# Earlier last loads, rested coefficient places and reordered adds at the end of a graph network's edge loop

## What the kernel computes

```python
msg = sum over b of (h[src] @ weight[b]) * w_comp[etype][:, b]     # 8 bases
x1  = layernorm(x + relu(segment_sum(msg * norm, dst) + bias))
rst = (1 + eps) * x1 + segment_sum(x1[src] + edge_attr, dst)
h   = relu(batchnorm(rst @ W1 + b1))                              # over all nodes
out = layernorm(x1 + h @ W2 + b2)
```

## Time and profile before

| What | us |
|---|---|
| median of 3 runs | 603.0 |
| lowest and highest | 601.1 and 605.9 |
| the profiled execution | 599.79 |
| its span | 598.0 |
| PE busy | 500.1 |
| DVE busy | 466.3 |
| POOL busy | 400.9 |
| mean granted PE clock | 0.905 of full |

### The profile page before, as it was taken

How to read it: one execution, slowest core, us unless ns; L and a number is a source line. 1 busy time by engine, 2 the same in 40 slices (tenths; PEclk the granted TensorE clock), 3 DMA queues, 4 the chain that set the end, 5 groups by cost and what they waited for, 6 DMA issues and landing times. The chain is left out here.

```text
span 598.0 us, 12928 instructions
## 1 busy us (share of the span) xinstructions
PE 500.1 (84%) x3981; PEld 425.1 (71%) x3981; DVE 466.3 (78%) x1835; ACT 219.9 (37%) x325; POOL 400.9 (67%) x434
## 2 busy tenths in 40 slices
PE   3779678898787987878978987968799999887995
PEld 2459578677677686766766876767788998875675
DVE  5999999999998697977599886798853564647566
ACT  8914546454333342333343342342400000002386
POOL 7777777777777777777777777777777777730000
PEclk9996988897877977879986997998999999898999
DMA  5423866576665665676666875685875596824003
GB/s 140 126 55 89 280 186 195 163 257 188 197 199 140 205 179 190 197 221 194 194 194 219 261 228 195 207 275 183 256 251 173 181 298 175 229 62 145 2 2 108
DMA packets 102010, 108.20 MB, mean 181 GB/s; under 512 B 11430, under 2 KB 89239, under 8 KB 101939
## 3 DMA queue, kind: packets, MB, share of 16 engines
q1 hardware_dynamic: 82658, 77.81, 39.8%
q0 software_dynamic: 13312, 27.29, 16.7%
q10 hardware_dynamic: 5968, 2.24, 1.5%
HBM read 81.74 MB, written 25.56 MB: 179 GB/s over the span
## 5 line engine op out<-in xcount | busy, mean ns | idle before, releaser
L862 POOL DMA_INDIRECT gathered_flat<-in_x_dram,src_i x402 | 385.2, 958 | 122.5 <-issue 90.2
L955 ACT ACTIVATE adj_flat<-psum 128x500 f16<-128x500 f32 (+1 forms) x208 | 127.4, 612 | 231.2 <-PE psum L1214 222.3
L1190 PE MATMUL psum<-weighted,gathered_flat 128*128 128x96 f32 (+1 forms) x808 | 143.9, 306 | 26.0 <-DMA gathered_flat<-in_x_dram,src_i 25.9
L1183 PEld LDWEIGHTS psum<-hot,attrs 128*128 128x128 f32 x832 | 147.7, 215 | 12.6 <-issue 9.7
L1190 PEld LDWEIGHTS psum<-weighted,gathered_flat 128*128 128x128 f32 x808 | 124.3, 215 | 30.5 <-DMA gathered_flat<-in_x_dram,src_i 30.4
L1681 DVE TENSOR_SCALAR etype_hot<-iota_key,key_t 128x300 f16<-128x300 f16 (+1 forms) x416 | 137.0, 331 | 0.0
L1183 PE MATMUL psum<-hot,attrs 128*128 128x12 f32 (+1 forms) x832 | 133.3, 237 | 2.4 <-DVE weighted L1562 2.4
L1214 PE MATMUL psum<-etype_hot 128*128 128x300 f16 (+1 forms) x416 | 131.3, 343 | 2.5 <-DVE etype_hot L1681 2.4
L1678 DVE TENSOR_SCALAR etype_hot<-iota_key,gathered_flat 128x128 f16<-128x128 f16 x416 | 106.4, 256 | 20.5 <-PE psum L1214 15.2
L1810 DVE TENSOR_TENSOR sums_flat<-psum,sums_flat 128x180 f32 x208 | 71.0, 341 | 24.6 <-PE psum L1183 3.9
L1758 DVE TENSOR_TENSOR sums_flat<-psum,sums_flat 128x132 f32 x160 | 45.0, 291 | 49.4 <-PE psum L1281 23.9
(11 more groups left out here) (168 smaller groups left out, 388.5 us busy)
## 6 DMA issues: line engine op xcount, KB each, us to landing
attrs<-in_edge_attr_dram SPq DMA_DIRECT2D x51, 512.0 KB
adjacency<-adj_flat SPq DMA_DIRECT2D x26, 900.0 KB
coef<-adjacency SPq DMA_DIRECT2D x26, 288.0 KB, 5.1
gathered_flat<-in_x_dram,src_i POOLq DMA_INDIRECT x402
sums_flat<-adjacency SPq DMA_DIRECT2D x9, 576.0 KB
sums_flat<-adjacency SPq DMA_DIRECT2D x13, 288.0 KB, 5.8
sums_flat<-adjacency SPq DMA_DIRECT2D x5, 432.0 KB, 5.5
sums_flat<-adjacency SPq DMA_DIRECT2D x4, 360.0 KB, 5.9
```

The costliest lines, as they stand in the source:

```text
L862: pool.indirect_dma_start(gathered_tile(t), None, x[:, :], bass.IndirectOffsetOnAxis((src_slots if t < AHEAD else src_i)[:, t:t + 1], 0)). ...
L955: nc.scalar.activation(window, counts, ACT.Copy).then_inc(counts_copied, 1)
L1183: product = nc.tensor.matmul(last_row(u, i), attrs[:, s * GROUP + j, :], hot_tiles(s, i)[:, u % GU, :], start=(u % 2 == 0 and i == 0), sto ...
L1190: nc.tensor.matmul(unit_psum(u)[:, 0:B, STARTS[i]:STARTS[i] + WIDTHS[i]], gathered_tile(u * UNIT + i), weighted_tiles(u // GU % 2, i)[:, u ...
```

## The change

It has five parts. (1) Six last loads in place of four are issued within the loop, one at each of steps 44 to 49, all into `sums`; a last buffer is as wide as the largest remainder (5 tiles, before 9). The load for place 12 then goes ahead of the rest, and no load but two waits for runs in `coef`. (2) In the final six units the planner uses no place in `coef`. (3) LATE_CUT moves from 3008 to 2976, and `late_bases(0)` waits for unit 199 (`added` of 200) and no more for unit 201. (4) The norm and split of part 8 stand between the adds of the finals, and the adds of a run after unit 207 ahead of part 7's norm. (5) By the planner's arithmetic there are now 59 runs, the same up to run 55. In the final six units there are three: run 56 after unit 202 (place 2), 57 after 203 (place 3) and 58 after 205 (place 0). None is after unit 207. There are 6 fills (blocks 3, 5, 8, 4, 10, 9), and of the 13 last products 11 have 3 tiles and 2 (blocks 12 and 11) have 5.

```diff
-    LATE_STEP = U - 6
-    LATE_CUT = LATE_AT + 3 * P // 2
+    LATE_STEP, LATE_DONE = U - 6, U - 8
+    LATE_CUT = LATE_AT + 5 * P // 4
...
-    FILL_MOST = 6
+    FILL_MOST, COEF_REST = 6, 6
...
-        if tiles <= CT:
+        if tiles <= CT and u < U - COEF_REST:
             places = [(NEARS + FARS + i, (i + 1) * FREE_COEF - 2) for i in range(COEFS)] + places
...
-    EARLY_LOADS, EARLY_STEP = 4, GROUPS - 6
+    EARLY_LOADS, EARLY_STEP = 6, GROUPS - 8
...
-        LAST_TILES = HIGHS - CHUNKS * CT + 2 * CT
+        LAST_TILES = HIGHS - min(first for _, first in LAST_RUNS)
...
-            if place < 4:
+            if place < 6:
                 return sums_rows(place % 2, 2 * RUN_WIDTH + place // 2 * LAST_WIDTH, tiles)
-            if place < 6:
-                return flat_rows(coef_flat, (place - 4) * 2 * LAST_WIDTH, tiles)
             if place < 8:
-                return sums_rows(place % 2, 0, tiles)
+                return flat_rows(coef_flat, (place - 6) * 2 * LAST_WIDTH, tiles)
...
-                    elif place < 6:
+                    elif place < 8:
                         sp.wait_ge(select_ready, GROUPS)
                         sp.wait_ge(nbr_mm, last_use(range(NEARS + FARS, NEARS + FARS + COEFS)))
-                    elif place < 8:
-                        sp.wait_ge(nbr_mm, last_use(range(NEARS + FARS)))
...
-                for b in LOAD_ORDER[EARLY_LOADS:6] + LOAD_ORDER[12:13] + LOAD_ORDER[6:12]:
+                for b in LOAD_ORDER[12:13] + LOAD_ORDER[6:12]:
                     load_last(b)
...
                     if u == LATE_STEP:
-                        pe.wait_ge(added, LATE_STEP)
+                        pe.wait_ge(added, LATE_DONE)
                         pe.wait_ge(x1_kept, LOOPED)
                         late_bases(0)
...
                 for k in LATE:
                     chunk_residual(k)
-                for k in LATE:
-                    chunk_norm(k)
-                    chunk_split(k, 0)
-                    chunk_split(k, 1)
                 if U - 1 in RUN_AT:
                     b = RUNS[-1][1]
                     for j in range(BLOCK):
                         add_run(NRUNS - 1, j, last_firsts[b * BLOCK:(b + 1) * BLOCK])
+                chunk_norm(LOOPED)
+                chunk_split(LOOPED, 0)
+                chunk_split(LOOPED, 1)
...
                 for n, (b, first, last) in enumerate(FINALS):
+                    if n == 2:
+                        chunk_norm(LOOPED + 1)
+                        chunk_split(LOOPED + 1, 0)
+                        chunk_split(LOOPED + 1, 1)
```

More of the change, by code:

```diff
@@ L102, in gnn_resnorm_kernel @@
     LATE = (LOOPED, LOOPED + 1)
-    LATE_STEP = U - 6
-    LATE_CUT = LATE_AT + 3 * P // 2
-    assert LATE_CUT < N and LATE_STEP % 2 == 0
+    LATE_STEP, LATE_DONE = U - 6, U - 8
+    LATE_CUT = LATE_AT + 5 * P // 4
+    assert LATE_CUT < N and LATE_DONE % 2 == 0
     assert max(PART_TILES) == CT and all(n % 2 == 0 for n in PART_TILES) and 0 < N - LATE_AT <= 512
@@ L154, in near_part, with places_for @@
         return max(k for k in range(LOOPED) if PARTS[k][0] < tiles * SPREAD // 2)
-    def places_for(tiles):
+    def places_for(tiles, u):
         places = [(i, split_step(near_part(tiles))) for i in range(NEARS)]
         places += [(NEARS + i, split_step(2)) for i in range(FARS)]
-        if tiles <= CT:
+        if tiles <= CT and u < U - COEF_REST:
             places = [(NEARS + FARS + i, (i + 1) * FREE_COEF - 2) for i in range(COEFS)] + places
@@ L194, in plan_runs @@
                 steps = [(max(opens, -(-used.get(place, 0) // 2), block_step(b)), i, place)
-                         for i, (place, opens) in enumerate(places_for(tiles(b, parts)))]
+                         for i, (place, opens) in enumerate(places_for(tiles(b, parts), u))]
                 step, _, place = min(steps)
@@ L424, in gnn_resnorm_kernel @@
         assert all(first >= HIGHS - LAST_TILES for _, first in LAST_RUNS) and len(LAST_RUNS) == 13
-        assert 2 * RUN_WIDTH + 2 * LAST_WIDTH <= LATE_AT and LAST_WIDTH <= 2 * RUN_WIDTH
+        assert 2 * RUN_WIDTH + 3 * LAST_WIDTH <= LATE_AT
         assert 4 * LAST_WIDTH <= T * B and COEFS * RUN_TILES <= T * B
@@ L746, in load_last @@
                     stored(b)
-                    if place < 4:
-                        covered = sum(first < 2 * RUN_WIDTH + 2 * LAST_WIDTH for first, _ in PARTS[:LOOPED])
+                    if place < 6:
+                        covered = sum(first < 2 * RUN_WIDTH + 3 * LAST_WIDTH for first, _ in PARTS[:LOOPED])
                         sp.wait_ge(x1_back, covered)
                         sp.wait_ge(parts_ready, covered)
-                    elif place < 6:
+                    elif place < 8:
                         sp.wait_ge(select_ready, GROUPS)
                         sp.wait_ge(nbr_mm, last_use(range(NEARS + FARS, NEARS + FARS + COEFS)))
-                    elif place < 8:
-                        sp.wait_ge(nbr_mm, last_use(range(NEARS + FARS)))
                     elif place == 12:
@@ L1603, in _ @@
             nc.vector.tensor_scalar(in_groups(excess[3]), behind, -1.0, None, ALU.mult)
-            nc.vector.tensor_scalar(excess[11], unit_row[:, LATE_STEP:LATE_STEP + 1], -1.0, float(LATE_CUT), ALU.mult,
+            nc.vector.tensor_scalar(excess[11], unit_row[:, LATE_DONE:LATE_DONE + 1], -1.0, float(LATE_CUT), ALU.mult,
                                     ALU.add)
```

## The result

| | before | after |
|---|---|---|
| median of 14 runs each, us | 602.45 | 598.43 |
| lowest and highest | 598.69 and 605.95 | 596.06 and 602.84 |
| ratio of the times | | 0.994, 95% interval 0.991 to 0.997 |
| the profiled execution | 599.79 | 596.44 |
| its span | 598.0 | 594.6 |

The changed kernel takes 4.0 us less (0.7%). The forecast was 4.2 us less and 598.8. The interval of the ratio stands for 1.9 to 5.3 us less, so that the times alone would also allow 2.5 us, the forecast's rival B; what tells them apart is the trace. The profiled executions are closer, 3.35 us, and the reader should see first why. Lines after L755 stand 4 lower in the changed kernel (L1810 is now L1806, L1281 is L1277, L1428 is L1424).

A forecast was written before the change was run, and what follows sets the result against it. The chain of waits between PE and DVE was taken to bound the kernel. Loop's end 2.94 us earlier, with tail gains and losses, summed to 4.2 us less: 598.8 against 603.0, range 595.5 to 603.0.

The forecast's parts named there:

- rival B: Tail: the TensorE clock falls once more after the two pauses; 2.5 us less in all, 600.5; chance 0.25.
- The loop's 2.94 us: Loop's end on DVE: couple 101 gains 0.83 us, couple 102 1.56, couple 103 0.55, so the loop ends 2.94 earlier.
- The late bases' wait: Ahead of the first late bases: PE no longer stands 0.99 us for unit 201; DVE's couple 101 gains 0.83 us.
- The wider second bases: Behind the loop: `late_bases(1)` goes from 117 to 149 columns, 0.35 us lost.
- The shorter first ones: First late bases: 160 columns in place of 192, 0.35 us less, 2.70 becoming 2.35 from start to start.
- The two loads at steps 44 and 45: Loop, steps 44 and 45: contention from two 360 KB loads taken as 0, at most 2.2 us in full.
- Rival D: Steps 44 and 45: gathers starve behind the added loads, 7.0 us lost against 4.2 won, 605.8; chance 0.06.
- The tail: From residual at 536.9 to the next product at 544.9, then 120 matmuls of 13.5 us; hidden layer at 558.5.
- The two pauses: Tail on PE: waits of 1.5 and 1.05 us with 0.7 us of work between, for three adds and part 8.
- The clock: Tail: full clock held likelier, as each pause is under 1.61 us; a fall would make the sum 2.5 us.
- Where the last gather landed: Loop's end: no gather packet behind 531.2, landing estimated at 531.7; DVE stays later than PE by 0.7 us.
- Rival C: Loop's end: unit 207's gathers land at 534, the loop's gain is not had; 1.3 us less, 601.7; chance 0.12.

The follow-up runs named there:

- e2: Changed kernel with part 2 undone: runs may use places in `coef` to the end, 62 runs; 600.89 us, ratio 0.997 to the kernel before.
- e1: Changed kernel with part 3 undone: the first late bases have 192 columns and wait for unit 201; 598.4 us, ratio 0.994 to the kernel before.
- e5: Kernel before with part 2 alone: no run of the last six units uses `coef`; 600.15 us, ratio 0.9986 to the kernel before.
- e3: Changed kernel with norm and split of parts 7 and 8 both ahead of all adds of finals; 599.07 us, ratio 0.9945 to the kernel before.
- e6: Changed kernel with norm and split of part 8 on POOL, the reciprocal kept on DVE; 598.99 us, ratio 0.9966 to the kernel before.
- e8: As e6, plus one fill added ahead of part 7's norm and window addresses read at couple 96; 598.26 us, ratio 0.9937 to the kernel before.
- e4: Changed kernel with four early loads, none at steps 44 and 45, nine behind the loop; 599.63 us, ratio 0.9947 to the kernel before.
- e7: Changed kernel without the eight gathers of units 120 to 123, so some output rows are wrong; 591.39 us, ratio 0.983.

## Why the prediction was right, and where it was not

**The loop's 2.94 us came out as summed**, 0.83, 1.57 and 0.55. The reader can see why such a sum can be exact: DVE's adds of a run wait for one another at 0.51 us, a register read costs 0.52 and a gap, and none of it has anything beside it at the end of the loop. e2 gives 1.56 and 0.55 back, e1 0.83. But the terms aren't independent, as the sum had them: e5 has the rested places without the earlier late bases and wins 0.21 of the 0.55, and e1 loses 0.33 in couple 103 beside its 0.83.

**The late bases' wait is a term only while PE is ahead.** In the changed kernel, e2, e3, e6 and e8 PE started them 0.25 us ahead of couple 100's adds and the whole 0.83 was had. In e4, where PE was late, 0.44 of it was left (4.25 against the 4.69 of e1), less the 0.28 for wider second bases: 0.16. I had priced this edit from one execution as if PE's lead were fixed. It varies by 1.2 us.

**The wider second bases** cost 0.28 in place of 0.35. The shorter first ones won more than the 0.35 of the sum: 160 columns took 2.17 from start to start, where I had 2.35. One price for each column doesn't hold: 2.04, 2.29, 2.34 and 2.87 us are the lengths at 117, 149, 160 and 192.

**The two loads at steps 44 and 45** cost nothing, as taken: 58.71 after, 58.77 without them, 58.85 before. Rival D is refuted here: PE waited for no gather between 465 and 490, and in no kernel that issues the loads is this stretch longer by anything near 7 us (58.7 to 59.3, and 60.2 in e1, whose half-clock stretch is twice as long as the changed kernel's). The Trainium skill (DMA: Bandwidth & Descriptors, "Queues, rings and completion order") says that each engine takes the queues with work in turn, by packets. The stretch that didn't get longer fits that, but no run here shows the order of the packets.

**The tail was 0.77 us cheaper than I summed.** From the residual to the next product I had 8.0 us (544.9 − 536.9) and it took 7.24. The split of part 8 ended 0.46 earlier relative to the residual than in my sum, as the three adds began while the split's last instruction ran out (542.57 against 542.23 + 0.42) and not 0.27 behind it. And the 0.3 us for the fifth add did not come: PE turned part 8 at 545.51 and went on at 545.71, since the fourth and fifth adds ran beside the third tile and the turning. The two pauses are real, 0.88 and 0.62 us for a predicted 1.5 and 1.05; each was overpriced, with the same mechanism. The 120 matmuls took 559.22 − 545.71 = 13.51, 13.5 in the sum.

**Part 4's order** had no term of its own in my sum. e3 gives it: 0.86 us.

**The clock.** Full clock in the tail is what I held likelier, and it is worth the 1.67 us of the earlier trace rows, two fifths of the forecast 4.2. A stretch from the changed kernel beside the last of the earlier trace rows (columns as there):

```profile
549.00:552.20 3.20, 3.20 (x31) 2.77 (x29) 1.86 (x9) 3.18 (x2) 0.00 (x0) 1.00 0.02 5
```

31 matmuls in the time of 17. But my reason, the length of the pause, falls. Behind pauses of 2.45 us (e2) and 2.53 (e5) the clock was at its lower level, 1.2 GHz; behind the same 2.53 in e3 it was at 2.4 GHz; in e3 two waits of 0.75 and 1.01 us with 0.8 us of work between were followed by 1.2 GHz; and a wait of 1.01 us ahead of the second late bases was followed by it in e7 (granted clock 0.57 from 527.3 to 531.3), but not in e1, e4 and e5. The Trainium skill (TensorE: Matmul & The Clock Gate, "What's actually happening") has half rate as the default that activity releases; that fits pauses being followed by it, but neither it nor my rule says which pause. Rival B didn't happen in this execution. No half-clock stretch stood behind the tail's pauses in the seven traces that have two short ones in place of a long one (the changed kernel, e1, e2, e4, e6, e7, e8); behind the long one it stood in two of three (the kernel before and e5, not e3). That speaks for the two pauses, but ten traces don't settle it. My forecast came out here because I chose between two values, not because I could tell which.

**Where the last gather landed.** I read from the kernel before that the gather queue has no packet behind 531.2, and carried over that the gathers are there by then. In the changed kernel POOL's last issue is 0.5 later, the queue has packets until 532.5, and SP, whose next load waits for this gather and nothing later, goes on at 532.98, 2.96 us behind the end of the issue. POOL's last issue, then the gather queue's row of the stretch from 532.25 to 532.5 (packets, MB, share of the engines):

```profile
529.08 0.94 POOL L858 DMA_INDIRECT gathered_flat<-in_x_dram,src_i  x1 [0.30 <-PE psum L1186]
```

```profile
q0 software_dynamic: 3, 0.00, 4.8%
```

In e3 the last packet lies at about 532.75 and SP goes on at 533.91, 3.78 us behind the end of the issue. In e8 it was 1.6 us at most (530.02 to 531.62, where SP was busy until just before). So the landing moves by over 2 us from one execution to the next, and the waiter goes on 0.5 to 1.1 us behind the last packet. The Trainium skill (DMA: Bandwidth & Descriptors, "Anatomy of one DMA — SWDGE (gpsimd) path") gives 2.0 us plus the bytes over 436 thousand per us, which makes an estimate of 2.15 us. That would be 532.2 in the changed kernel; the waiter is later there and in e3, and earlier in e8. Rival C's mechanism therefore exists: in the changed kernel the gathered product of unit 207 starts at 533.01, right behind the landing, 0.56 us behind the attribute products ahead of it, where 0.38 is usual; in e3 it starts at 533.94 and costs 0.43. The profile puts DVE's last idle time of 0.44 us down to PE, but e6 and e8 have the same 1.28 or 1.27 us with DVE as the releaser, and the chain of waits of the changed kernel runs through DVE's register read there:

```profile
533.83 0.20 DVEq L1744
```

PE had ended unit 207 by 533.85, and in e3, where DVE did wait for PE, its adds start 0.13 us behind that end. So PE was in time by some 0.3 us: 533.85 + 0.13 against 534.27. I had 0.7. The term came out, with less to spare than I summed; a DVE faster by more than 0.3 us at this place would have won nothing.

**Sum.** Predicted 4.2 in the profiled execution; measured 4.98 in M, less 1.63 lost ahead of it, where I find no edit at work, 3.35; by the medians 4.0. That the median came within 0.2 us of the forecast is in part luck: the tail was 0.77 us cheaper, the interval is 1.9 to 5.3, and a fall of the clock costs 1.6. The parts of M: from the kernel before to e5 the coefficient places give 1.65; from e5 to the changed kernel M falls by 3.33, which is 0.89 for the late bases (e1), 0.86 for the order of adds (e3), 0 for the early loads (e4) and 1.57 for the half clock in e5's tail. That makes 4.97 of M's 4.98, of which 3.40 are the edits' and the rest the clock's. Where PE is late at the late bases (e4), 0.73 of the 0.89 isn't had.

## What to carry to other kernels

At the end of a loop where two engines hand work to each other, write down for each handover how far ahead the waited-for engine is and what else could be late next (here the last gather): a saving counts only up to that floor. Two savings of one handover aren't independent either: ask for each what is left of it without the other. Where the clock costs 1.6 us at a time and comes at changing places, compare kernels by the same stretch, piece by piece, and take the half-clock pieces out first; the 0.86 us of e3 stood in a difference of medians of 0.6, with 1.8 of uncertainty. Read a landing from several executions where there are any, and from what the waiter does, for here it moves by 2 us.

## What the runs showed of the hardware

- An indirect gather of 128 rows takes POOL 0.94 us and then a gap of 0.30, also where nothing is to be waited for (POOL's rows at 524.08, 525.33, 526.58 are 1.25 apart). Busy shares hide the gap: from 490 to 500, where it issues one after the other, POOL shows as busy for 7.56 us of 10.00.
- From the end of the issue of the last gather until its waiter goes on it took 2.96 us in the changed kernel, 3.78 in e3 and at most 1.6 in e8, of nearly the same program; its last packet was 0.5 and 1.1 us ahead of that in the first two.
- On 53x128 tiles POOL needs 1.05 us for a norm with two column scalars (DVE 0.34), 0.52 to 0.55 for a conversion (0.22) and 0.42 for a difference (0.28).
- The same pause of 2.53 us was followed by the lower clock in one kernel (e5) and by the full one in another (e3), and a wait of 1.01 us at the same place by the lower one in e7 and by the full one in e1, e4 and e5. What decides isn't settled by these runs.
